# Last expert layer of a six-stage macaron block: the sorted order cut into four segments of tokens, the final gathers, sums and stores moved between the later blocks

## What is computed

```python
def _L1_ffn_ref(x, router_w, w1, w2):         # N = 8192 tokens, E = 8 experts, top 2
    capacity = int(1.25 * N * 2 / E) + 1
    probs = softmax(xf @ router_w.T)
    k_probs, k_idx = top_k(probs, 2)          # then divided by their sum
    rank = position of the (token, choice) pair among the pairs of its expert, in token order
    keep = rank < capacity
    h = silu(buf @ w1[e]); out_buf = h @ w2[e]     # 128 -> 512 -> 128, per expert
    combined = sum over the 2 choices of out_buf[expert, slot] * keep * k_prob
    return combined + x
x = x + 0.5 * _L1_ffn_ref(_layernorm(x), ...)
```

## Time and profile before

| | us |
|---|---|
| three runs, median (lowest, highest) | 3590.76 (3590.43, 3595.3) |
| the profiled execution | 3593.5 |
| its span, first to last instruction | 3591.7 |
| routing of the last layer, up to its first block load | about 3056 to 3147 |
| its 71 blocks | 3147 to 3421 |
| `add_and_store` | 3425 to 3592 |

### The profile page before, as it was taken

One profiled execution on the slowest core, in us unless ns is written; L12 is line 12 of the kernel. 1 busy time (PEld: TensorE's weight loads), 2 busy tenths in 40 slices (PEclk: granted clock), 3 DMA queues, 4 the chain that ended last, 5 costly groups with the idle time before them and its releaser, 6 DMA issues. The chain is left out here.

```text
span 3591.7 us, 45021 instructions
## 1 busy us (share of the span) xinstructions
PE 2679.7 (75%) x12336; PEld 1880.9 (52%) x12336; DVE 2211.8 (62%) x3886; ACT 1544.3 (43%) x2662; POOL 2124.8 (59%) x1697
## 2 busy tenths in 40 slices
PE   4699995997579998449983767867867866599900
PEld 4599982443468897429981322322322323389900
DVE  4766553675566564673320989989989887733312
ACT  4333334663433333423334556546646633433300
POOL 0477761322057776335544988988888685355467
PEclk9899996777589999559996889999999998599955
DMA  6011112000401111602232877878877876122222
GB/s 170 18 47 47 46 40 58 24 24 1 124 28 47 45 47 32 188 9 70 70 71 63 277 264 267 278 255 273 286 243 267 280 251 195 31 64 71 69 69 76
DMA packets 286348, 429.39 MB, mean 120 GB/s; under 512 B 58332, under 2 KB 195839, under 8 KB 286240
## 3 DMA queue, kind: packets, MB, share of 16 engines
q1 hardware_dynamic: 250784, 357.34, 30.2%
q0 software_dynamic: 35456, 70.86, 8.3%
HBM read 367.51 MB, written 62.39 MB: 120 GB/s over the span
## 5 line engine op out<-in xcount | busy, mean ns | idle before, releaser
L600 POOL DMA_INDIRECT m_rows<-rows_in,m_source x568 | 552.0, 972 | 361.8 <-PE m_T_ps L628 211.5
L1497 PE MATMUL s_y_ps<-s_prod,ident 128*128 128x512 f32 x1024 | 549.0, 664 | 281.1 <-DVE s_prod L1766 281.0
L1759 DVE TENSOR_TENSOR_SCAN s_dA<-s_dA,s_dBu 128x1024 f32<-128x1024 f32 x256 | 586.2, 2290 | 146.4 <-POOL s_dBu L1457 72.3
L1457 POOL TENSOR_TENSOR s_dBu<-s_du,s_B_row 128x1024 f32<-128x1024 f32 x256 | 602.8, 2358 | 104.5 <-DVE s_dA L1759 97.0
L634 PE MATMUL m_A_ps<-m_rowsT,m_own 128*128 128x256 f32 x2272 | 566.5, 382 | 2.0 <-ACT m_rowsT L681 1.1
L650 PE MATMUL m_Y_ps<-m_own,m_hid 128*128 128x128 f32 x4544 | 554.3, 275 | 3.6 <-issue 3.6
L650 PEld LDWEIGHTS m_Y_ps<-m_own,m_hid 128*128 128x128 f32 x4544 | 529.8, 192 | 5.7 <-issue 5.6
L1497 PEld LDWEIGHTS s_y_ps<-s_prod,ident 128*128 128x128 f32 x1024 | 192.0, 205 | 600.4 <-DVE s_prod L1766 404.7
L634 PEld LDWEIGHTS m_A_ps<-m_rowsT,m_own 128*128 128x128 f32 x2272 | 412.9, 192 | 48.3 <-ACT m_rowsT L681 1.9
L1587 ACT ACTIVATE s_dA<-s_delta,s_decay 128x1024 f32<-128x1024 f32 x256 | 285.6, 1118 | 336.3 <-DVE s_prod L1766 329.7
L691 ACT ACTIVATE m_act_a<-m_A_ps,m_own 128x256 f32<-128x256 f32 x568 | 238.5, 471 | 433.8 <-PE m_A_ps L634 302.5
(11 more groups left out here) (229 smaller groups left out, 3789.0 us busy)
## 6 DMA issues: line engine op xcount, KB each, us to landing
s_B_row<-s_bc_rows SPq DMA_DIRECT2D x256, 512.0 KB, 5.6
s_C_row<-s_bc_rows SPq DMA_DIRECT2D x256, 512.0 KB, 5.7
rows_out<-m_y_sb SPq DMA_DIRECT2D x142, 128.0 KB, 1.9
rows_in<-m_xs SPq DMA_DIRECT2D x64, 256.0 KB, 3.2
m_rows<-rows_in,m_source POOLq DMA_INDIRECT x568, 2.5
s_got<-rows_by_token SPq DMA_DIRECT2D x16, 512.0 KB, 5.1
m_got<-rows_by_token SPq DMA_DIRECT2D x32, 256.0 KB, 4.2
rows_by_token<-m_y_sb,m_target POOLq DMA_INDIRECT x284, 2.3
```

The costliest lines, as they stand in the source:

```text
L600: pool.indirect_dma_start(rows[:, b % 2, r, :], None, c.rows_in, bass.IndirectOffsetOnAxis(source[:, 2 * b + r:2 * b + r + 1], 0)).then_in ...
L1457: nc.gpsimd.tensor_tensor(dBu[q % RING][:, :], du[s % 2][:, h, :], B_row[q % RING][:, :], ALU.mult).then_inc(dBu_ready, 1)
L1497: ins = nc.tensor.matmul(y_ps[:, at(cc, 512)], c.ident[:, :], prod[q % 2][:, at(cc, 512)], start=(n == 0), stop=(n == NS - 1))
L1759: nc.vector.tensor_tensor_scan(dA[q % 2][:, :], dA[q % 2][:, :], dBu[q % RING][:, :], 0.0, ALU.mult, ALU.add).then_inc(scanned, 1)
```

## The change

`moe` gets two parameters, `cuts` and `out`; the last layer is called with `cuts=(16, 32, 48)` and `out=out`, and `add_and_store` is gone. With S = 4 segments the sorted order is by segment of 16 token tiles, and by expert within one. Each expert's count up to a segment's end is rounded up to whole blocks (`upto`), and the difference to the segment before is that expert's share of the segment (`size`), so that the 71 blocks stay 71. For the other layers S is 1, which leaves them one copy more (`size`).

```diff
+                for i, end in enumerate(ends):
+                        link(nc.vector.tensor_scalar(upto_i[:, i, :], cum[:, :, end - 1], float(CAP), float(BLK - 1), ALU.min, ALU.add))
...
+                link(nc.vector.tensor_copy(size[:, 0, :], upto[:, 0, :]))
+                if S > 1:
+                    link(nc.vector.tensor_tensor(size[:, 1:S, :], upto[:, 1:S, :], upto[:, 0:S - 1, :], ALU.subtract))
...
+                link(nc.vector.tensor_tensor(offset[:, :, :], run_end[:, :, :], upto[:, :, :], ALU.subtract))
+                if S > 1:
+                    link(nc.vector.tensor_tensor(further[:, 1:S, :], offset[:, 1:S, :], offset[:, 0:S - 1, :], ALU.subtract))
...
+                for i in range(1, S):
+                    link(nc.vector.tensor_tensor(over[:, :, :], cum[:, :, :], over_tiles(upto[:, i - 1, :]), ALU.is_ge))
+                    link(nc.vector.tensor_tensor(shifted[i % 2][:, :, :], over[:, :, :], over_tiles(further[:, i, :]), ALU.mult))
+                    if i > 1:
+                        link(nc.vector.tensor_tensor(shifted[i % 2][:, :, :], shifted[0][:, :, :], shifted[1][:, :, :], ALU.add))
+                if S > 1:
+                    link(nc.vector.tensor_tensor(cum[:, :, :], cum[:, :, :], shifted[(S - 1) % 2][:, :, :], ALU.add))
...
-                link(nc.vector.tensor_tensor(passed[:, :, :], c.block_row[:, :].unsqueeze(2).to_broadcast([P, NBLK + 2, E]),
-                                             run_end[:, :].unsqueeze(1).to_broadcast([P, NBLK + 2, E]), ALU.is_ge))
+                link(nc.vector.tensor_tensor(passed[:, :, :], c.block_row[:, :].unsqueeze(2).to_broadcast([P, NBLK + 2, S * E]),
+                                             run_end[:, :, :].rearrange("p i e -> p (i e)").unsqueeze(1).to_broadcast([P, NBLK + 2, S * E]),
+                                             ALU.is_ge))
                 link(nc.vector.tensor_reduce(bmap[:, :], passed[:, :, :], AX.X, ALU.add))
+                for i in range(1, S):
+                    link(nc.vector.tensor_scalar(round_done[:, :], bmap[:, :], float(E), float(-E), ALU.is_ge, ALU.mult))
+                    link(nc.vector.tensor_tensor(bmap[:, :], bmap[:, :], round_done[:, :], ALU.add))
...
+            LEAD = 3
+            RINGS = 8
+            full_at = [(2 * P * end + E * (BLK - 1)) // BLK for end in ends]
+            turn_of, tile_at = {}, 0
+            for b in range(NBLK if out is not None else 0):
+                part = next((i for i, end in enumerate(ends) if tile_at < end))
+                if b >= full_at[part] + LEAD and tile_at < NT:
+                    turn_of[b], tile_at = tile_at, tile_at + 1
+            late_tiles = range(tile_at, NT)
...
+            def get_rows(pool, t):
+                part = next(i for i, end in enumerate(ends) if t < end)
+                if t == 0 or t in ends:
+                    for u in range(2):
+                        pool.wait_ge(y_stored[u], (full_at[part] + 1 - u) // 2 * 16)
+                wait(pool, mine_added, (t - RINGS + 1) * 2)
+                for k in range(2):
+                    pool.indirect_dma_start(mine[:, t % RINGS, k, :], None, c.rows_out,
+                                            bass.IndirectOffsetOnAxis(get_i[k][:, t:t + 1], 0)).then_inc(mine_here[t % RINGS], 16)
+
+            def add_rows(dve, t):
+                dve.wait_ge(mine_here[t % RINGS], (t // RINGS + 1) * 32)
+                for k in range(2):
+                    if k == 1:
+                        dve.wait_ge(mine_added, t * 2 + 1)
+                    nc.vector.scalar_tensor_tensor(
+                        out=c.x[:, at(t), :], in0=mine[:, t % RINGS, k, :].unsqueeze(1), scalar=weight[k][:, at(t)],
+                        in1=c.x[:, at(t), :], op0=ALU.mult, op1=ALU.add).then_inc(mine_added, 1)
...
                     load(b)
...
+                    if b in turn_of:
+                        get_rows(pool, turn_of[b])
+                if out is not None:
+                    for t in late_tiles:
+                        get_rows(pool, t)
...
+                    for b in range(NBLK):
+                        step(b, b % 2, first=(b == 0), last=(b == NBLK - 1))
+                        if b - 1 in turn_of:
+                            add_rows(dve, turn_of[b - 1])
                 finish(NBLK - 1, 0)
+                if out is not None:
+                    if NBLK - 1 in turn_of:
+                        add_rows(dve, turn_of[NBLK - 1])
+                    for t in late_tiles:
+                        add_rows(dve, t)
...
+                        for b in range(NBLK):
+                            store(b, b % 2)
+                            if b - 3 in turn_of and (turn_of[b - 3] + 1) % GRP == 0:
+                                send_x(sp, sent)
+                                sent += 1
+                        for g in range(sent, NG):
+                            send_x(sp, g)
+                        sp.wait_ge(x_stored, NG * 16)
...
+                 lambda: moe1("m2", rows_before=True), lambda: scan1("s1"), lambda: moe1("m3", cuts=(16, 32, 48), out=out)]
...
-        add_and_store(nc, c, "last", out, by_token=False)
```

More of the change, by code:

```diff
@@ L148, in _, with moe @@
             nc.vector.tensor_copy(c.beyond[:, :], beyond_i[:, :])
-def moe(nc, c, tag, gated, w, rows_before=False, by_token=False):
+def moe(nc, c, tag, gated, w, rows_before=False, by_token=False, cuts=(), out=None):
     PACK = 3 * F + 2 * FC + D if gated else 2 * F
@@ L160, in moe @@
     B2 = W2 + F
+    ends = tuple(cuts) + (NT,)
+    S = len(ends)
     with ExitStack() as ctx:
@@ L222, in moe @@
             place = rsb("place", [P, NT, E])
-            over = None if gated else rsb("over", [P, E, NT])
+            shifted = [rsb(f"shifted{i}", [P, E, NT]) for i in range(2)] if S > 1 else None
+            over = rsb("over", [P, E, NT])
             ind = rsb("ind", [P, NT])
@@ L227, in moe @@
             cum = rsb("cum", [P, E, NT])
[L228 to L231, removed]
+            upto = rsb("upto", [P, S, E])
+            upto_i = rsb("upto_i", [P, S, E], I32)
+            size = rsb("size", [P, S, E])
+            run_end = rsb("run_end", [P, S, E])
+            offset = rsb("offset", [P, S, E])
+            further = rsb("further", [P, S, E])
             bmap = rsb("bmap", [P, NBLK + 2])
-            passed = rsb("passed", [P, NBLK + 2, E])
+            passed = rsb("passed", [P, NBLK + 2, S * E])
+            round_done = rsb("round_done", [P, NBLK + 2])
             tps = [rc.enter_context(nc.psum_tensor(f"{tag}_tps{u}", [P, GRP * P], F32)) for u in range(2)]
@@ L372, in _ @@
                                                   tot_ps[:, :], 0.0, ALU.mult, ALU.add))
[L373 to L376, removed]
+                for i, end in enumerate(ends):
+                    if gated:
+                        link(nc.vector.tensor_scalar(upto_i[:, i, :], cum[:, :, end - 1], float(BLK - 1), None, ALU.add))
+                    else:
+                        link(nc.vector.tensor_scalar(upto_i[:, i, :], cum[:, :, end - 1], float(CAP), float(BLK - 1), ALU.min, ALU.add))
@@ L381, in _ @@
[L381 to L382 removed]
+                link(nc.vector.tensor_copy(upto[:, :, :], upto_i[:, :, :]))
+                link(nc.vector.tensor_copy(size[:, 0, :], upto[:, 0, :]))
+                if S > 1:
+                    link(nc.vector.tensor_tensor(size[:, 1:S, :], upto[:, 1:S, :], upto[:, 0:S - 1, :], ALU.subtract))
@@ L775, in _ @@
                     select_bias(0, 0, e0)
[L776 to L781, removed]
-                finish(NBLK - 1, 0)
+                if out is None:
+                    step(0, 0, first=True)
+                    step(1, 1)
+                    with dve.Fori(0, (NBLK - 3) // 2) as i:
+                        step(i * 2 + 2, 0)
+                        step(i * 2 + 3, 1)
+                    step(NBLK - 1, 0, last=True)
+                else:
+                    for b in range(NBLK):
+                        step(b, b % 2, first=(b == 0), last=(b == NBLK - 1))
+                        if b - 1 in turn_of:
+                            add_rows(dve, turn_of[b - 1])
+                finish(NBLK - 1, 0)
+                if out is not None:
+                    if NBLK - 1 in turn_of:
+                        add_rows(dve, turn_of[NBLK - 1])
+                    for t in late_tiles:
+                        add_rows(dve, t)
             @block.sync
@@ L789, in _ @@
                 if not by_token:
-                    two_slot_loop(sp, NBLK - 1, store)
-                    store(NBLK - 1, 0)
+                    if out is None:
+                        two_slot_loop(sp, NBLK - 1, store)
+                        store(NBLK - 1, 0)
+                    else:
+                        sent = 0
+                        for b in range(NBLK):
[6 more added lines that the diff above has]
+                        sp.wait_ge(x_stored, NG * 16)
                     for u in range(2):
@@ L1784, in _ @@
```

17 lines of the change are left out of this document (13 added, 4 removed).

## The result

| | before | changed |
|---|---|---|
| median (lowest, highest), first comparison | 3590.89 (3590.43, 3595.3) | 3550.52 (3544.74, 3552.36) |
| ratio, 95% interval | | 0.9878 (0.9865, 0.989) |
| median in the second comparison (e1_again) | 3593.91 | 3542.46, ratio 0.9856 (0.984, 0.9873) |
| span of the profiled execution | 3591.7 | 3550.1 |
| clearing of the semaphores ahead of the last layer, to the end | 565.7 | 519.4 |

What follows compares the result with a forecast made beforehand. PE was taken to bound the last layer's blocks and POOL the tail; 13.4 + 54.4 - 2.1 - 120.0 - 1.7 + 1.3 = -54.7 us from 3591.7 gave a span of 3537.0, forecast 3536 us, range 3522 to 3562.

Steps and rivals of the forecast that it cites:

- last transposes to the first of the last gathers: Tail: gather 48 starts 11.7 us after the last transposes, where the first gather before started 13.8 after: -2.1 us.
- from the last gather to the end: Tail's close: last sum of one tile instead of four, -1.7 us; closing barriers behind the last store, +1.3 us.
- Routing: Last layer's serial DVE chain grows: +7.7 us before the marks, +5.1 behind; other expert layers +0.6; +13.4 in all.
- Blocks: Blocks 26 to 70: four indirect DMAs make POOL the bound at 5.00 us a block against PE's 3.74; +54.4 us.
- an indirect DMA costs POOL 1.25 us wherever it stands: Blocks and tail: each indirect DMA takes POOL 0.94 us busy plus 0.30 issue gap, in both stretches.
- The waits of the segments: POOL's gathers wait for block 22's store, counted in the sum; the two other segment waits should cost nothing.
- The tail: After the last blocks, 32 gathers at 1.25 us stand where 128 stood: -120.0 us.
- one block end of some 0.7 was there anyway: Closing barriers: at most 2.2 us, with a block end of some 0.7 already present before, so +1.3 us.
- Hidden gathers: Rival, blocks: POOL issues two more DMAs inside PE's 3.74 us, the 54.4 mostly falls away; 3482 us, chance 0.04.
- The dearer gather: Rival, blocks: DVE's work slows POOL's issue, 0.13 us more for 180 DMAs; 3559 us, chance 0.13 with lasting segment waits.
- The clock: Rival, blocks: PE's idle gaps lower TensorE's clock, block 7.5 us; 3648 us, chance 0.09, of which 0.05 slower than before.
- The segments: Rival, blocks: segment waits met late hold up loads, up to 20 us; 3556 us, chance 0.13 with the dearer gather.

Runs made afterwards that it cites:

- e1_again: The changed kernel run once more without edits: 3542.46 us against 3593.91 before, ratio 0.9856; last layer 519.4 us.
- e10_narrow_dve: Changed kernel with DVE's sums cut to one channel and weight copies to 8 columns from block 2 on: last layer 515.3 us.
- e6_spread_padding: Changed kernel with the last layer's padding rows gathering different rows instead of all row 0: 3547.36 us, ratio 0.9864; last layer 517.6 us.
- e3_one_gather: Changed kernel with one gather behind each load from block 26 on instead of two: 3539.86 us, ratio 0.985; last layer 511.4 us.
- e7_early_cuts: e3_one_gather with cuts at tiles 5, 15, 35 instead of 16, 32, 48: 3529.38 us, ratio 0.982; last layer 498.3 us.
- e9_early_no_drain: e7_early_cuts without the last layer's closing POOL drain, barriers and semaphore clearing: 3521.93 us, ratio 0.9805; last layer 495.2 us.

## Why the prediction held, point by point

The time lay in the range and above the forecast: 3550.5 and 3542.5 against 3536. The layers ahead moved by 8 us from one profile to the next, so how near the whole time came is in part luck; the last layer's gain is the fair test, and it was 46.3 us where the terms give 55.3, 9.0 too much. The two steps below, in the blocks (5.2) and in the tail (3.5), make up nearly all of that. By its own terms, in us, from the two first profiles:

| term | predicted | measured |
|---|---|---|
| layers ahead of the last | +0.6 | +4.6 (e1_again: -3.5) |
| last layer to the first transposes | +12.8 | +12.9 |
| blocks 0 to 24 | 0 | +0.3 |
| blocks 24 to 70 | +54.4 | +59.6 |
| last transposes to the first of the last gathers | -2.1 | -2.2 |
| 96 gathers fewer behind the blocks | -120.0 | -120.0 |
| from the last gather to the end | -0.4 | +3.1 |

*Routing.* Right in both halves: +7.9 us ahead of the marks for +7.7, +5.2 behind them for +5.1. An operation with a broadcast operand costs 0.69 us like the others (L406 below, beside L408 without one), so the 2 us held for it were not needed:

```profile
3104.00 0.69 DVE L406 TENSOR_TENSOR m_shifted<-m_over,m_further 128x512 f32<-128x512 f32 x1
3104.72 0.69 DVE L408 TENSOR_TENSOR m_shifted<-m_shifted 128x512 f32<-128x512 f32 x1
```

*Blocks.* The mechanism was right, POOL the bound from block 28 on, and the term 5.2 us too small. The step "an indirect DMA costs POOL 1.25 us wherever it stands" is the one: between these blocks it cost 1.268, which over 43 blocks is 3.2 us. The prediction took 1.25 since loads in the same blocks showed it beside DVE's copies; but POOL was idle for part of each block there and is never idle now, so more of its DMAs can meet a copy; this reason is argued. e10_narrow_dve gave 1.248 with most of DVE's work left out. 1.6 us are the last load's landing, for which I took the gathers' median of 2.5 us; e6_spread_padding shows the padding as the cause of 1.3 of them. The remaining 0.4 lie in the first wait.

*The waits of the segments.* Right: the only waits of POOL for stores were 2.27 us at block 26 and 5.00 us at tile 48; at blocks 42 and 58 there were none. The prediction had the second one too, as 11.7 against 8.3 us after the transposes, but said that nothing is lost by it. Measured against what was possible something was: e3_one_gather, where other gathers fill it, has no such wait.

*The tail.* 32 gathers at 1.25 us, as forecast. The closing barriers and the clearing took 1.4 us for the forecast 1.3, but POOL's drain ended 3.5 us after the last store was seen. The step "one block end of some 0.7 was there anyway" failed: here the block's end came with POOL's drain, at 3548.7, and rows 5 don't hold that drain. Between the last gather and the end the sum had 0.4 us less than before; it was 3.1 more.

*Rivals.* Hidden gathers (3482): excluded. One gather a block more makes a block 0.06 us longer (e3_one_gather, 3.79 for 3.73), two make it 1.34 us longer (the changed kernel, 5.07); the rule of the Trainium skill that descriptor generation is small ("DMA: Bandwidth & Descriptors", section "Anatomy of one DMA — SWDGE (gpsimd) path") doesn't hold for these gathers, at 0.94 us of POOL each. The dearer gather: true in kind, DVE's copies beside POOL, at 0.018 us a DMA and not 0.13. The clock: it read 1.00 over 120 us with PE busy for 78% and idle about 1.1 us a block, and 0.96 over the next 80; it didn't decide anything. The segments: no wait at the second and third.

## What to carry to other kernels

When work moves from a tail to a stretch with another bound, count what the moving engine can do per turn there: only its idle time in that stretch is won, and everything past it comes back as a delay of what stood behind it in its queue. Here 1.24 us a block was free, one gather fits and two don't, and both kernels hide about the same amount; so the gain grows with how early the first gather may go (cuts at 5, 15, 35), not with gathers beyond the one a block that fits. Compare executions from a marker ahead of the changed stage: the last layer came out the same to 0.1 us in the two profiles of the changed kernel, and its blocks to 1 us in four, where the whole kernel moved by 8.

## What the runs showed of the hardware that I had not expected

- POOL's drain at a block's end took until 8.4, 7.2 or 6.3 us after its last indirect DMA with 270 of them in the block (changed kernel, e3_one_gather, e7_early_cuts), and 2.9 us with 128 in the kernel before. Leaving it and the closing barriers out was worth 5.3 us in the changed kernel and 3.1 in e9_early_no_drain.
- The last load, in which padding rows all read one row, lands 1.0 to 1.3 us later than one in which they read different rows: 3.86 to 4.13 against 2.85 us to the transposes.
- A DVE operation with two SBUF inputs of 0.77 us took 2.64 us when it started beside a 2.46 us product on POOL, and one of 0.20 us with a single input took 2.07 (L437 of the changed kernel, at 3152.21).
- With DVE's copies and sums made small, indirect DMAs are 0.01 to 0.03 us shorter in the mean (953 to 943 ns for a load, 977 to 944 for a gather); the step from 967 to 944 is the copies'.
- The gated scan took 343.3 and 339.7 us in two executions of the same code, and 339.3 to 344.3 over all profiles; what sets it stays open.
